# First sequence's residual, norm and turning moved beside the backward scan; the second's kept in stage 3

## What is computed

```python
def _mamba2(x, in_w, conv_w, ...):              # once forward, once on flip(x)
    z, xBC, dt = split(x @ in_w.T)
    xBC = silu(depthwise_conv(xBC, conv_w))      # 4 taps
    S_t = S_{t-1} * exp(dt * A) + dt * x_t B_t   # the scan over time, 8 heads
    y = (S_t C_t + Dp * x) * silu(z)
    return rmsnorm(y) @ out_w.T
mixed = mamba2(x, fwd) + flip(mamba2(flip(x), bwd))
x1 = x + layernorm(mixed)                        # the residual
src = layernorm(x1)
q, k, v = src @ q_w, src @ k_w, src @ v_w        # 16 heads of 16
scores = (q k^T) / 4 * (2 * sigmoid(q . scale_w))
attn = softmax(scores) v                         # then gate, projection, norm, top-2 router, experts
```

## Time and profile before

| | us |
|---|---|
| median of 3 runs | 2645.15 (2643.93 to 2647.07) |
| the profiled execution | 2645.64, span 2643.8 |
| busy | PE 2446.9 (93%), DVE 2102.7 (80%), ACT 1769.8 (67%), POOL 983.8 (37%) |

### The profile page before, as it was taken

One profiled execution on the slowest core, in us unless ns is written; L12 is line 12 of the kernel. 1 busy time (PEld: TensorE's weight loads), 2 busy tenths in 40 slices (PEclk: granted clock), 3 DMA queues, 4 the chain that ended last, 5 costly groups with the idle time before them and its releaser, 6 DMA issues. The chain is left out here.

```text
span 2643.8 us, 44996 instructions
## 1 busy us (share of the span) xinstructions
PE 2446.9 (93%) x16296; PEld 1087.2 (41%) x16296; DVE 2102.7 (80%) x4197; ACT 1769.8 (67%) x2295; POOL 983.8 (37%) x1152
## 2 busy tenths in 40 slices
PE   6799999999657999999999999999999999786995
PEld 6366666666443222222222222222232232573553
DVE  4577777787665999999989899898999993593885
ACT  2578777777321577788778787787787888212663
POOL 1377787777650122222121221122210111344664
PEclk9899999999876899999999999999999999877998
DMA  2222232222232030313004012030030000215884
GB/s 89 90 82 76 89 98 84 81 84 84 68 118 56 13 61 14 53 21 53 10 13 61 13 33 30 14 61 7 7 61 2 1 2 1 95 57 210 287 286 143
DMA packets 111282, 179.23 MB, mean 68 GB/s; under 512 B 18796, under 2 KB 85764, under 8 KB 105796
## 3 DMA queue, kind: packets, MB, share of 16 engines
q1 hardware_dynamic: 102724, 158.21, 22.3%
q0 software_dynamic: 6016, 15.41, 1.5%
q10 hardware_dynamic: 2320, 2.74, 0.3%
HBM read 149.47 MB, written 31.21 MB: 68 GB/s over the span
## 5 line engine op out<-in xcount | busy, mean ns | idle before, releaser
L1435 DVE TENSOR_REDUCE max_part<-round_psum 128x1 f32<-128x512 f32 x2048 | 1267.8, 683 | 101.4 <-PE round_psum L1360 97.2
L1404 ACT ACTIVATE p_exp<-score_psum 128x1024 f32<-128x1024 f32 x1024 | 993.3, 1022 | 215.3 <-PE score_psum L1347 210.5
L1360 PE MATMUL round_psum<-k_stack,q_stack 64*128 64x512 bf16 x2048 | 722.2, 390 | 20.4 <-DMA k_stack<-qk_rows 12.7
L1338 PE MATMUL score_psum<-q_stack,k_stack 64*128 64x512 bf16 x2048 | 599.7, 379 | 0.9 <-ACT p_exp L1404 0.2
L1347 PE MATMUL score_psum<-q_stack,k_stack 35*128 35x512 bf16 x2048 | 594.9, 378 | 0.0
L1380 PE MATMUL pv_psum<-p_exp,values 128*17 128x512 f32 x4096 | 539.7, 598 | 0.0
L1360 PEld LDWEIGHTS round_psum<-k_stack,q_stack 64*128 64x128 bf16 x2048 | 191.4, 94 | 624.7 <-DVE max_part L1435 521.8
L559 PE MATMUL rot<-tokens_t,w_in 128*128 128x512 f32 x576 | 274.1, 604 | 15.9 <-DVE bc_conv L697 12.3
L1347 PEld LDWEIGHTS score_psum<-q_stack,k_stack 35*128 35x128 bf16 x2048 | 189.0, 94 | 116.4 <-issue 0.8
L1469 POOL TENSOR_TENSOR rden<-pv_out,minus_one 128x16 f32<-128x16 f32 x32 | 92.8, 2901 | 358.5 <-ACT pv_out L1419 356.2
L1338 PEld LDWEIGHTS score_psum<-q_stack,k_stack 64*128 64x128 bf16 x2048 | 139.5, 94 | 59.4 <-ACT p_exp L1404 26.3
(11 more groups left out here) (251 smaller groups left out, 3549.3 us busy)
## 6 DMA issues: line engine op xcount, KB each, us to landing
expert_w<-in_expert_w SPq DMA_DIRECT2D x39, 1028.0 KB, 5.6
cum_rows_in<-cum_rows SPq DMA_DIRECT2D x64, 512.0 KB, 3.9
cum_pairs_in<-cum_rows SPq DMA_DIRECT2D x120, 128.0 KB, 3.6
qk_rows<-qk_parts SPq DMA_DIRECT2D x64, 192.0 KB, 3.1
q_stack<-qk_rows SPq DMA_DIRECT2D x84, 128.0 KB, 7.7
k_stack<-qk_rows SPq DMA_DIRECT2D x84, 128.0 KB, 8.7
token_rows<-tokens SPq DMA_DIRECT2D x16, 512.0 KB, 3.1
x_in<-in_x SPq DMA_DIRECT2D x8, 512.0 KB, 8.6
```

Source lines behind the costliest of these rows:

```text
L1338: nc.tensor.matmul(ebank[i // 2][:, i % 2, :], ks[rows, n % 2, plane, k * P:(k + 1) * P], qs[rows, n % 2, plane, q * BLK:(q + 1) * BLK], s ...
L1360: nc.tensor.matmul(bank[step][:, :], qs[rows, n % 2, plane, at:at + P], ks[rows, n % 2, plane, keys * BLK:(keys + 1) * BLK], start=True, s ...
L1404: nc.scalar.activation(pt[:, (k * 2 + pair) % 4, :, :], ebank[pair][:, :, :], ACT.Exp).then_inc(*exped.up(u, k, pair))
L1435: nc.vector.tensor_reduce(mx[:, c * HG + h, keys:keys + 1], bank[step][:, :], AX_X, ALU.max).then_inc(*maxed.up(u, k, i))
```

## The change

**In the backward scan** each chunk r of the first sequence (counted as it comes, chunk c = 15 - r) gets its residual and its second norm one chunk at a time, from round q = 36 to 65 (`RES_AT`, 16 of them, every 7/4 rounds: 36, 37, 39, 41, 43, 44, 46, 48, ... 60, 62): `r_stat`, `r_root`, `r_norm` in that round, `r_add`, `s_stat`, `s_root` one later, `s_norm` two later, `s_turn` and `s_copy` three later. `s_turn` takes a turn in the ring of the three `rot` banks, and `s_copy` writes into `tokens_t` over columns that the scan no longer reads. SyncE loads x and saves x1 chunk by chunk (`rows_on_sync`). The backward half gets its own four orders for each engine.

**Stage 3** keeps blocks 4 to 7 and gets an order for each engine (`STAGE3`). The split of the first group reads only the first sequence, so it no longer waits for any norm. The weights are loaded on SyncE's queue, those of group 0 first. The values of chunks 0 to 15 are projected here.

**In attention's lead** each of the first 16 steps projects the values of one of the chunks 16 to 31, into score banks that are still free, and ACT stores them. The first score matmul waits for the last of them.

```diff
+RES = SEQ // P
+RES_AT = {NQ // 2 + CPB + r * 7 // 4: r for r in range(RES)}
+RES_LAG = {"r_stat": 0, "r_root": 0, "r_norm": 0, "r_add": 1, "s_stat": 1, "s_root": 1, "s_norm": 2, "s_turn": 3,
+           "s_copy": 3}
...
+           "s_turn across products tile0 tile1 rows",
+           "s_turn across products tile0 tile1 rows",
+           "s_turn products across tile0 tile1 rows",
+           "tile0 across tile1 products tile2 s_turn rows"),
...
+            "r_stat across out products s_stat m s_norm gate r_norm mean tile0 tile1",
+            "across r_stat out products s_stat m s_norm gate r_norm mean tile0 tile1",
+            "r_stat across products out gate s_stat s_norm m r_norm mean tile0 tile1",
+            "r_stat across gate out products s_stat s_norm m mean r_norm tile2 tile0 tile1"),
...
+            "tile0 s_copy out decays tile1 spread",
+            "spread s_copy out tile0 decays tile1",
+            "spread s_copy out tile0 decays tile1",
+            "silu_z silu_x out tile0 tile1 skip tile2 s_copy decays spread"),
...
+             "out r_add decays r_root products s_root state c gate",
+             "out r_add decays r_root products state s_root c gate",
+             "out decays state products r_add c r_root gate s_root",
+             "out decays r_add products r_root state c gate s_root"),
...
+            elif what in RES_LAG:
+                if q - RES_LAG[what] in RES_AT:
+                    yield what, 0, RES_AT[q - RES_LAG[what]]
...
+    def rows_on_sync(sp_, q):
+
+
+        for r in chunks:
+            c = RES - 1 - r
+            if ends[r] + 2 == q:
+                if r >= 2:
+                    sp_.wait_ge(*x1.at(r - 2))
+                nc.sync.dma_start(x_res[:, r % 2, :], xv[:, c, :]).then_inc(*x_load[r % 2].up(r))
+            if ends[r] + 7 == q:
+                sp_.wait_ge(*x1.at(r))
+                nc.sync.dma_start(x1_dram[:, c, :], acc[:, c, :]).then_inc(*x1_saved.up("chunk", r))
...
+                if what == "s_turn":
+                    r = x
+                    pe.wait_ge(*src_in.at(r))
+                    pe.wait_ge(*bank_read(*before["src", r]))
+                    for k in range(KD):
+                        t = nc.tensor.transpose(bank["src", r][:, k * P:(k + 1) * P], src[:, two, k * P:(k + 1) * P],
+                                                K["ident"])
+                    t.then_inc(*src_turned.up(r))
...
+                if what == "s_copy":
+                    r, c = x, RES - 1 - x
+                    act.wait_ge(*src_turned.at(r))
+                    act.wait_ge(*columns_read(r))
+                    nc.scalar.copy(xnT[:, :, c * P:(c + 1) * P],
+                                   heads(bank["src", r][:, 0:D], KD, P)).then_inc(*src_stored.up(r))
...
+                if what == "r_stat":
+                    ve.wait_ge(*acc_dve.at(NQ // 2 + r))
+                    var_on_vector(nc, ve, own, lambda i: acc[:, c, :], stat[:, one, :], mv[:, one, :], rstd[:, one], 1,
+                                  mixed_var.up(r))
+                if what == "r_norm":
+                    ve.wait_ge(*mixed_rstd.at(r))
+                    nc.vector.tensor_scalar(acc[:, c, :], acc[:, c, :], mv[:, two, 0:1], rstd[:, one], ALU.subtract,
+                                            ALU.mult).then_inc(*normed.up(r))
+                if what == "s_stat":
+                    ve.wait_ge(*x1.at(r))
+                    var_on_vector(nc, ve, own, lambda i: acc[:, c, :], stat2[:, one, :], src_mv[:, c:c + 1, :],
+                                  src_rstd[:, c:c + 1], 1, src_var.up(r))
+                if what == "s_norm":
+                    ve.wait_ge(*src_root.at(r))
+                    if r >= 2:
+                        ve.wait_ge(*src_turned.at(r - 2))
+                    nc.vector.tensor_scalar(src[:, two, :], acc[:, c, :], src_mv[:, c, 0:1], src_rstd[:, c:c + 1],
+                                            ALU.subtract, ALU.mult).then_inc(*src_in.up(r))
...
+                if what == "r_root":
+                    po.wait_ge(*mixed_var.at(r))
+                    rsqrt_on_pool(nc, rstd[:, two:two + 1], K["power"], 1, mixed_rstd.up(r))
+                if what == "r_add":
+                    po.wait_ge(*normed.at(r))
+                    po.wait_ge(*x_load[two].at(r))
+                    nc.gpsimd.tensor_tensor(acc[:, c, :], acc[:, c, :], x_res[:, two, :], ALU.add).then_inc(*x1.up(r))
+                if what == "s_root":
+                    po.wait_ge(*src_var.at(r))
+                    rsqrt_on_pool(nc, src_rstd[:, c:c + 1], K["power"], 1, src_root.up(r))
...
+STAGE3 = {
+    "SP": "weights0 load4 weights1 fill load7 load5 keep4 load6 save0 keep5 stack0 save1 stack1 keep6 keep7",
+    "PE": "project00 project01 scale0 project10 values0 project11 values1 values2 turn4 scale1 turn5 values3 "
+          "turn6 turn7",
+    "ACT": "project00 project01 scale0 high0 values0 low0 values1 turn4 project10 values2 project11 scale1 high1 "
+           "low1 turn5 turn6 turn7 values3",
+    "DVE": "mixed4 mixed5 residual4 residual5 mixed6 source4 multiply0 source5 residual6 mixed7 turn4 residual7 "
+           "source6 source7 multiply1 turn5 turn6 turn7",
+    "POOL": "mixed4 mixed5 residual4 scale0 multiply0 mixed6 residual5 high0 low0 source4 mixed7 residual6 "
+            "source5 residual7 scale1 multiply1 source6 source7 high1 low1",
+}
...
+                if what == "weights":
+                    g = slice(0, 1) if b == 0 else slice(1, NG)
+                    nc.sync.dma_start(S.w_qk[:, :, g, :], io["w_qk"][:, :, g, :]).then_inc(*S.loaded[b].up(0))
+                    if b == 0:
+                        nc.sync.dma_start(S.w_sc, io["w_sc"]).then_inc(*S.scale_loaded.up(0))
+                        nc.sync.dma_start(w_v, io["v_w"]).then_inc(*w_load.up(0))
...
+            if left == ("max", 2) and t + LEAD < NCH // 2:
+                yield "values", NCH // 2 + t + LEAD, 0, 0
...
+                if what == "values":
+                    c = u
+                    if c - 4 in late:
+                        pe.wait_ge(*v_stored.at(c - 4))
+                    for kd in range(KD):
+                        m = nc.tensor.matmul(v_bank(c), S.srcT[:, kd, c * P:(c + 1) * P], S.w_v[:, kd, :],
+                                             start=(kd == 0), stop=(kd == KD - 1))
+                    m.then_inc(*v_summed.up(c))
                 if what == "turn_rows":
...
+                if what == "values":
+                    act.wait_ge(*v_summed.at(u))
+                    nc.scalar.copy(V[:, u, :, 0:HD], heads(v_bank(u), AH, HD)).then_inc(*v_stored.up(u))
```

More of the change, by code:

```diff
@@ L373, in mamba_order @@
         n, j = divmod(q, CPB)
-        for what in STEPS[engine][j].split():
+        for what in STEPS[engine][j + (CPB if q >= NQ // 2 else 0)].split():
             if what in AHEAD:
                 yield from chunk(what, q + AHEAD[what])
+            elif what in RES_LAG:
+                if q - RES_LAG[what] in RES_AT:
+                    yield what, 0, RES_AT[q - RES_LAG[what]]
             elif what.startswith("tile"):
@@ L455, in mamba @@
     follow = [q for q in range(NQ) if not starts(q)]
-    bank = {u: rot[i % 3] for i, u in enumerate(tiles)}
-    before = {u: tiles[i - 3] for i, u in enumerate(tiles) if i >= 3}
+    users = [(n if what == "project" else "src", x) for what, n, x in order["PE"] if what in ("project", "s_turn")]
+    bank = {u: rot[i % 3] for i, u in enumerate(users)}
+    before = {u: users[i - 3] for i, u in enumerate(users) if i >= 3}
     halves = [slice(r * NST, (r + 1) * NST) for r in range(2)]
@@ L541, in _ @@
                                       ).then_inc(*pair_load[q % 2].up(q, r))
+            for q in range(NQ, NQ + CPB + 4):
+                rows_on_sync(sp_, q)
         @block.tensor
@@ L871, in __init__ @@
         halves = [(n, j) for n in range(len(GROUPS)) for j in range(2)]
-        self.loaded = sems.dma("w_qk_load", range(2))
+        self.loaded = [sems.dma(f"w_qk_load{i}", [0]) for i in range(2)]
+        self.scale_loaded = sems.dma("w_sc_load", [0])
         self.filled = sems.dma("rows_fill", [(slot, odd) for slot in range(2) for odd in range(2)])
@@ L994, in stack_on_sync, with stage3_step @@
                               rows[odd]).then_inc(*S.stacked[slot].up(n, j, t, kind, odd))
+STAGE3 = {
[9 more added lines that the diff above has]
+}
+def stage3_step(word):
+    what, at = word.rstrip("0123456789"), [int(i) for i in word.lstrip("abcdefghijklmnopqrstuvwxyz")]
+    if what == "stack":
+        return [(what, 0, at[0], t) for t in range(TERMS)]
+    if what in ("project", "scale", "multiply", "high", "low", "save"):
+        return [(what, 0, *at, *[0] * (2 - len(at)))]
+    return [(what, *at, *[0] * (3 - len(at)))]
 def residual_and_values(nc, sems, ctx, K, io, mixed, srcT, S, V, src_mv, src_rstd, x1_dram, x1_saved):
@@ L1015, in residual_and_values @@
     xv = io["x"].rearrange("b (c p) d -> p (b c) d", p=P)
```

(30 more changed lines are left out.)

123 lines of the change are left out of this document (74 added, 49 removed).

## The result

The changed kernel takes **2606.65 us** (median of four, 2603.85 to 2614.66), where the kernel before, run beside it, takes 2645.42: a ratio of 0.9858, 95% interval 0.9836 to 0.9881. The forecast was 2613, in a range from 2594 to 2638. The profiled execution took 2603.85 us with a span of 2602.0, 41.8 us less than the span before.

The account below looks back on a forecast made before the run. PE bounds the backward scan, a DVE chain its last chunks, and order rather than an engine stage 3. Stage 3 -49, lead -3, scan +20 make -32 on 2645.6: 2613.6, median 2613 us, range 2594 to 2638.

Parts of the forecast that it names:

- the second half's own chain: Stage 3: second-half steps from turning through norms, copies and POOL to saves and stacks set the stage's end, saving 49 us.
- T + 61: Stage 3: predicted time of the first maximum, counted from the stage's start T = 0, against 109.6 us before.
- SyncE's floor: Stage 3: save1 stands behind stack0, so the second half can't be done before T + 55, 57 to the first maximum.
- PE without a pause: Lead: at half clock PE would have no pause, so full clock comes after a few steps, at a cost of 2 us.
- The waits for POOL: Scan: four TENSOR_SCALARs a chunk wait for POOL at the shared port, 0.35 us each, making DVE's load 3.8 a chunk.
- what doesn't fit under the idle time of its own window: Scan: DVE's added work beyond each window's idle time, summed over rounds 36 to 58, is 19 us, taken as 13.
- The tail term: Scan's last rounds (60 to 64): DVE's added steps stand in the chain itself and cost 5 us.
- Rival 1: The scan hides the work in position 3's idle time: scan +8, stage 3 -52, total 2598; chance 0.20.
- Rival 2: The scan clogs, DVE nearly full and tile work standing behind r_norm: scan +40, total 2634; chance 0.17.
- Rival 3: Stage 3's single orders wait for each other, it stays near 80 us and saves 30: total 2632; chance 0.08.
- Rival 4: Scan: DVE and POOL wait for each other at their port, setting the pace: scan +61, total 2654; chance 0.08.
- positions 0 and 2: Scan windows of a four-chunk block where DVE idles only 1.04 and 0.31 us; the unhidden cost was to fall there.

Follow-up runs that it names:

- the warm lead: Changed kernel with nine unused chunks of value matmuls added at the end of PE's stage-3 list: 2603.52 us, ratio to before 0.9849.
- the fourth kernel: Changed kernel with each of the 32 statistics taken twice, 13.3 us more for DVE: 2614.8 us.
- the old orders: Changed kernel with the backward half's orders of the kernel before, the new words put into them: 2649.18 us, ratio to before 1.0007.
- the order alone: Kernel before with the backward half's new orders and none of the residual's steps: 2651.77 us, where before took 2649.21.
- the combination: Changed kernel with second-sequence values projected in stage 3 and the k half of stack1 on ScalarE's queue: 2619.15 us, ratio 0.9902.
- the other kernel: Changed kernel with the k half of stack1 (12 transfers) issued on ScalarE's queue, the q half on SyncE's: 2612.75 us.

## Why the prediction was right, point by point

**Stage 3 (forecast -49, measured -53.6).** The mechanism held: the second half's own chain sets the end, as walked. The stacks on SyncE aren't unbroken: the first half's were issued by 758.4, `save1` waited for POOL's `low1` and went out at 760.38. That is T + 38, where I had T + 43; from there on the walk fits, 5.0 us to the stacks, 11.1 of issue and 2.1 to the first maximum. So T + 61 came out as 56.1, the term being too long by the 5 us that I gave too much to the norms, copies and powers ahead of `low1`. Even SyncE's floor of T + 57 was beaten by 1, as the first half's stacks began at T + 25 instead of T + 28; 1.2 us of that is a slip of adding (3, 3.5 and 1.75 make 8.25, where I wrote 9.5). The floor's reason was half of it: with one queue the issue does end within 2 us of the landing, but halving it gained nothing, as the transfers were a second floor of the same height.

**The lead (forecast -3, measured +1.9 in the first profile and +5 in the second).** The term was mis-sized, inside my -5 to +6. Full clock did come, and with it the `project` steps became short (1.96 us), but only after three steps or more of 3.94 us where DVE needs 2.4. I had allowed 2 us for the slow start; it cost 4.1 and 7.2 in the two profiles, against the warm lead. The warm lead's 53.5 us gains 2.2 on before's 55.7, where I had counted on 4 to 5 from the `project` steps. "PE without a pause" was no reason for full clock: the lead of the kernel with the values in stage 3 has PE busy for 51.2 of 56.1 us and stays at 0.59. The Trainium skill's "TensorE: Matmul & The Clock Gate", section "What's actually happening", ties the clock to PE's recent activity. These two leads are about equally busy in the records (50.1 of 57.6 us and 51.2 of 56.1) and have different clocks (0.86 and 0.59), so the busy share of a profile could not have told me which I would get.

**The scan (forecast +20, measured +9.6).** Here two prices were too high and one too low. The waits for POOL were too dear. Groups of the changed kernel's scan (busy us, mean ns):

```profile
L118 DVE BATCH_NORM_STATS2 c_stat<-tokens 128x6 f32<-128x256 f32 x32 | 13.3, 417 | 0.0
...
L856 DVE TENSOR_SCALAR src_chunk<-tokens,src_mv,src_rstd 128x256 f32<-128x256 f32 x16 | 11.9, 742 | 0.0
...
L846 DVE TENSOR_SCALAR tokens<-tokens,c_mv,c_rstd 128x256 f32<-128x256 f32 x16 | 8.4, 527 | 0.0
```

And one line's durations over that scan (min/median/max ns):

```profile
L127 DVE TENSOR_SCALAR c_rstd<-c_mv x16: 153/153/154, 449.9 to 700.8; 128x1 f32<-128x1 f32 x16
```

`r_norm` and `s_norm` lose 0.12 and 0.34 us to such waits, as the earlier trace rows had it; the two TENSOR_SCALARs over one column lose nothing in 32 cases, 28 of which began inside an instruction of POOL. That is 0.46 a chunk where I took 1.4, and 2.8 us of DVE a chunk instead of 3.8. With the Trainium skill's "SBUF — State Buffer", section "Who interferes with whom", I had called all four waits real. The section has `tensor_scalar` contend only when its operands meet certain conditions, which I passed over. Here the wide ones waited and the narrow ones didn't.

The next step, that what doesn't fit under the idle time of its own window is paid in full (19, taken as 13), was too strict: by the fourth kernel more work on DVE comes out at 0.43 on the us. My 9 us for idle time shared within a block was wrong too: by the same loads and idle times it is under 5. From q = 36 to 59 the steps cost 5.5 instead of 13, the turning the 2.0 that I took. The other way went what I had costed at nothing: the order of the lists, +2.0. The tail term (+5) came out as +0.7 from q = 60 to the last `out`, but before's profile was at 0.78 in its last 14 us and after's at 1.00, which is worth 1.5 to 2.5 us by my estimate (the changed kernel itself took 12.5 us from q = 63 on at 1.00 in its first profile, and 15.0 in its second, where the clock had fallen); so up to 3 us of it may be real.

**The rivals.** Rival 1 (scan +8, stage 3 -52) came closest to the terms: 9.6 and 53.6. Its price of 2598 supposed the lead's gain too, which didn't come. So the time lies between that rival and the forecast: against the forecast the scan is 10.4 us cheaper, stage 3 is 4.6 shorter and the lead 4.9 longer, and the other stretches together make +0.3. That is 9.8 us under the forecast for the profiled execution; the median lies 2.8 above that execution, so 6 under. That the number came so near is in part luck: the lead's error took back half of the scan's. Rival 2's picture, tile work on DVE behind the norms, is what the old orders give (+47.5 on the scan, where rival 2 had +40), and the new ones avoid. Rival 3: no. Rival 4: no loop over the port; POOL's busy time from 430 to 684 rose from 196.57 to 213.35 us, and no wait of PE for it shows.

**The signs.** Windows longer in positions 0 and 2, with PE under their length: no. Longer are 1 and 2 (10.1 to 10.4 and 9.9 to 10.8 us, 9.07 and 9.16 before), 3 is shorter (9.5 to 9.7, 10.98 before), and PE is busy in most of them; the order alone gives the same picture (9.07, 10.13, 9.92, 9.51). `across` released by DVE's `gate` or decay: once between 487 and 670, by `gate`, 1.1 us; else in the last rounds. The last `out` 20 us later: 7. TENSOR_SCALARs above 0.6: 0.63 on the mean of both. Lead above 0.9 and under 56 us: no, 0.86 and 57.6.

## What to carry to other kernels

When work is moved into a loop that one engine fills, the order of the queues can decide more than the work: here the same steps cost 9.6 us of scan in one arrangement and 47.5 in another, which ate the whole gain, while the better order alone would have looked like a loss. So cost the order and the load as a pair. Where a phase starts after PE has idled, some matmuls of no use at the end of the idle phase can be the cheapest work of the kernel (9 chunks took 1 to 7 us off this lead, by how late the clock rose without them); first see in the trace that the phase loses steps at 1.2 GHz, and that its own load keeps the clock up afterwards. This burst of transfers, whose issue and whose transport take about equally long, gained nothing from a second queue, and in the combination the engine that lent the queue paid.

## What the runs showed of the chip

- The granted clock and the busy share go apart: 18.5 busy us of 20 at clock 0.59 (maxima of 64x512 bf16 only), 32.0 of 37 at 1.00 (the same maxima with 128x256 f32 projections between them).
- A TENSOR_SCALAR on 128x1 took 153 to 155 ns in all 32 cases, 28 of them begun inside an instruction of POOL; on 128x256 it took from 403 to 1505, the long ones begun inside one.
- 24 transfers of 64 KB from device memory: the step that needs them started 13.2 us after the first issue from one queue and 13.7 from two, with a median from issue to landing of 2.2 to 2.3 and of 5.7 to 6.1 us.
- Issuing 11 DMAs took ScalarE's queue 6.62 us, 0.6 each, in which its copies stood still (12 took 5.59 us in the other kernel).
